# A mixture-of-experts stage: twelve of its 32 token tiles sent through DRAM to their two experts

## The reference, cut to what matters

```python
h = _layernorm(x) * (1 + ca) + sa                 # second layer
z = softmax(einsum('bse,he->bsh', h, W_A) * SCALING, axis=1)
out = causal_convolution(z, h @ W_V.T)            # per head, over all positions
x = x + ga * (out @ W_O.T + b_O)
h = _layernorm(x) * (1 + cb) + sb
weights = softmax(h @ gate_w.T)                   # 16 experts
top2_w, top2_idx = top_k(weights, 2)
y = relu(einsum('nh,edh->ned', h, expert_w) + expert_b)     # all 16 experts
x = x + gb * sum(take(y, top2_idx) * top2_w)                # two of them count
```

## Time and profile before

| | us |
|---|---|
| median of 3 runs | 1114.5 (1114.38 to 1114.91) |
| the profiled execution | 1114.68 |
| its span, first to last instruction | 1112.9 |
| mean granted clock of PE | 0.990 |

### The profile page before, as it was taken

The page is one execution under the profiler, slowest core; times in us unless marked ns, Lnnn a source line. Parts: engine busy times, 40 slices in busy tenths (PEclk is TensorE's granted clock), DMA queues, the critical chain, the costliest instruction groups (busy, mean ns, idle before and its releaser), DMA issues. The chain is left out here.

```text
span 1112.9 us, 34196 instructions
## 1 busy us (share of the span) xinstructions
PE 1034.9 (93%) x11851; PEld 716.1 (64%) x11851; DVE 870.4 (78%) x2888; ACT 840.4 (76%) x2673; POOL 735.5 (66%) x1184
## 2 busy tenths in 40 slices
PE   6889998799999999898899999998998999999995
PEld 3667764477777776565577777776565598854442
DVE  4999997588888888564788888887685653379998
ACT  5789984699999998433799999997355855478986
POOL 4999995699898897201888988987233220046775
PEclk9999999899999999999999999999999999899999
DMA  7000000112222221321112221221001444000000
GB/s 250 5 3 12 12 3 1 39 40 61 57 54 53 51 49 39 111 73 31 40 39 50 49 49 40 50 49 42 21 1 41 105 122 107 3 8 15 17 20 19
DMA packets 66509, 51.02 MB, mean 46 GB/s; under 512 B 42263, under 2 KB 53443, under 8 KB 66051
## 3 DMA queue, kind: packets, MB, share of 16 engines
q1 hardware_dynamic: 66339, 48.84, 17.3%
HBM read 21.41 MB, written 2.38 MB: 21 GB/s over the span
## 5 line engine op out<-in xcount | busy, mean ns | idle before, releaser
L1259 PE MATMUL psum<-wa_wqkv,wa_hT 128*128 128x512 f32 x384 | 189.0, 600 | 1.3 <-DVE wa_tmp L1124 1.3
L1216 ACT ACTIVATE wa_p<-psum,wa_nb 128x128 f32<-128x128 f32 x512 | 184.7, 403 | 0.0
L1105 POOL TENSOR_TENSOR wa_p<-wa_p,wa_rrs 128x512 f32<-128x512 f32 x128 | 133.4, 1042 | 10.1 <-DVE wa_rrs L1149 10.1
L1140 DVE CUSTOM_DVE_ANT_0 psum<-psum,wa_bias 128x128 f32<-128x128 f32 x512 | 132.5, 322 | 5.8 <-PE psum L1297 5.8
L1216 ACT ACTIVATION_READ_ACCUMULATOR wa_p<-psum,wa_nb 128x1 f32 x512 | 125.0, 244 | 0.0
L1997 ACT ACTIVATE cv_z_ex_yw<-psum,ex_w 128x128 f32<-128x128 f32 x384 | 106.9, 411 | 16.3 <-POOL ex_topf L1829 4.4
L2067 PE MATMUL psum<-ex_wc,ex_hT 128*128 128x512 f32 x256 | 115.8, 600 | 2.4 <-DVE cv_z_ex_yw L1932 1.4
L1081 POOL TENSOR_TENSOR wa_kr<-wa_kr,wa_tmp 128x512 f32<-128x512 f32 x64 | 81.7, 1276 | 41.6 <-DVE wa_tmp L1124 41.6
L1092 POOL TENSOR_TENSOR wa_qr<-wa_qr,wa_rn 128x512 f32<-128x512 f32 x64 | 66.8, 1044 | 56.3 <-ACT wa_rn L1198 56.3
L1226 ACT ACTIVATE wa_pT<-psum 128x512 f32<-128x512 f32 x128 | 78.3, 612 | 31.8 <-PE psum L1273 31.7
L1124 DVE TENSOR_TENSOR wa_tmp<-psum,wa_tabs 128x512 f32<-128x512 f32 x128 | 87.2, 681 | 0.0
(11 more groups left out here) (265 smaller groups left out, 3031.0 us busy)
## 6 DMA issues: line engine op xcount, KB each, us to landing
wa_vm<-wa_v SPq DMA_DIRECT2D x127, 128.0 KB, 2.4
cv_toep<-cv_zpad SPq DMA_DIRECT2D x32, 136.0 KB, 2.9
cv_toep<-cv_zpad SPq DMA_DIRECT2D x16, 264.0 KB, 4.4
wa_tabs<-in_rotations_dram SPq DMA_DIRECT2D x2, 2048.0 KB, 7.9
wa_rows<-y_rows SPq DMA_DIRECT2D x31, 128.0 KB
wa_rows<-y_rows SPq DMA_DIRECT2D x31, 127.0 KB
x_rows<-in_L_attn_x_dram SPq DMA_DIRECT2D x4, 512.0 KB, 5.6
out_dram<-x_rows SPq DMA_DIRECT2D x32, 64.0 KB, 1.5
```

The costliest lines, as they stand in the source:

```text
L1105: nc.gpsimd.tensor_tensor(p, p, cols_bc(rrs[:, t % 2, r, :], P), ALU.mult)\
L1140: m = nc.vector.tensor_tensor_reduce(out=s, in0=s, in1=edges, scale=-1.0, scalar=MAX_FLOAT, op0=ALU.add, op1=ALU.min, accum_out=nb[:, t % ...
L1216: e = nc.scalar.activation(pr[:, t % 2, r, h, :], sim_bank[r][:, P * h:P * h + P], ACT.Exp, bias=nb[:, t % 2, r, h:h + 1], scale=-1.0, acc ...
L1259: nc.tensor.matmul(bank, hT[:, t % 3, :], wqkv[:, INNER * k:INNER * k + INNER], start=True, stop=True).then_inc(done.sem, 1)
```

## The change

Tiles 0 to 11 (`SPARSE = 12`) no longer pass through all 16 experts. Each token is copied to two rows of a table in DRAM, one per chosen expert, the table is multiplied block by block with the expert that owns the block, and each token reads its two result rows back.

- POOL clears 35 semaphores at the start of the block (`ro.all`), makes constants (`fixed`), and normalises the twelve tiles in row form (`routed_rows`).
- PE turns those rows in convolution step 7 (`routed_turn`, 12 transposes) and multiplies them with the gate (`routed_gate`, 12 matmuls of 16 columns) into bank 7. To have them ready, `o_project` and `turn_o` of batch 0 are moved into steps 5 and 6, two groups each, all through bank 6.
- DVE takes top values and indices of the twelve tiles (`choose`, before it takes away the last convolution step) and marks them (`mark`). PE counts each token's rank in its expert (`ranks`, 13 matmuls), DVE turns it into a row number (`place`, 8 operations), into the expert of each block (`columns_of_weights`) and makes the two weights (`two_weights`).
- SP writes zeros over the table, 2.6 MB (`zero`). POOL sends the rows out in 24 indirect transfers (`scatter`, from step 9 of its phase). The table has 40 blocks of 128 rows, taken four at a time: 10 quads. SP fetches for each quad the rows in one transfer and the four expert matrices in four, each with a column number that it loads from SBUF into a register (`routed`), into three slots. PE transposes a quad, ACT copies it, PE multiplies it (four matmuls of 128x128), DVE takes relu times gb, SP stores the result. Two quads pass in each of the steps 17 to 21, between the dense `up` matmuls.
- POOL reads the results back in 24 indirect transfers (`gather`, from step 22, behind the store of all quads), DVE adds them with their weights (`sums`, steps 24 to 29).
- The dense experts have 20 tiles (12 to 31) instead of 32; `EARLY` is 2 instead of 6. The five choice stages of the dense tiles run on DVE, and the eight compares of a group are one.

The core of the diff:

```diff
+SPARSE = 12
+SCATTER_FROM, SCATTERS_PER = 9, 5
+QUADS_FROM, QUADS_PER = 17, 2
+GATHER_FROM, GATHERS_PER, SUM_LAG = 22, 2, 2
+        def routed(sp):
+            weights_ready(sp, 0)
+            sp.wait_ge(ro.v_meta, META_DONE)
+            sp.wait_ge(ro.scattered, 16 * 2 * SPARSE)
...
+            for q in range(NQ):
+                slot = q % ro.SLOTS
+                if q >= ro.SLOTS:
+                    sp.wait_ge(ro.p_up, q - ro.SLOTS + 1)
+                sp.dma_start(ro.rows_in[slot], rows[q]).then_inc(ro.fetched[slot], 16)
+                for i in range(4):
+                    at = sp.value_load(ro.column[0:1, 4 * q + i:4 * q + i + 1], min_val=0, max_val=(NE - 1) * E)
+                    sp.dma_start(ro.weights_in[slot][:, i, :], wc[:, 0, bass.ds(at, E)])\
+                      .then_inc(ro.fetched[slot], 16)
+                if q >= ro.SLOTS:
+                    result(q - ro.SLOTS)
...
+            def scatter(s):
+                for j, k in scatter_at.get(s, []):
...
+                    nc.gpsimd.indirect_dma_start(
+                        out=ro.hs, out_offset=bass.IndirectOffsetOnAxis(ap=ro.pos[:, j, k:k + 1], axis=0),
+                        in_=ro.y[:, j, :], in_offset=None).then_inc(ro.scattered, 16)
+            def gather(s):
+                for j in gather_at.get(s, []):
+                    if j == 0:
+                        gp.wait_ge(ro.stored, 16 * NQ)
...
-            return Phase([of(floats, 5), of(numbers_equal, 5), of(either, 5), of(masked, 6), of(weights, 6),
-                          (residual, UP_LAG + 2)], 0, TILES)
+            return Phase([(residual, UP_LAG + 2), step_from(scatter, SCATTER_FROM),
+                          step_from(gather, UP_LAG + 2)], 0, DENSE)
...
+            def quad_turn(n):
+                def f(s):
+                    for q in quads_at.get(s, [])[n:n + 1]:
+                        turn_bank_left(pe, "quad", q)
+                        pe.wait_ge(ro.fetched[q % ro.SLOTS], 80 * (q // ro.SLOTS + 1))
+                        for i in range(4):
+                            m = nc.tensor.transpose(h_bank[:, P * i:P * i + P], ro.rows_in[q % ro.SLOTS][:, i, :],
+                                                    c.ident[:, :])
+                        m.then_inc(ro.p_quad, 1)
+            def quad_up(n):
...
+                        pe.wait_ge(ro.a_quad, q + 1)
...
+                        for i in range(4):
+                            m = nc.tensor.matmul(bank[:, P * i:P * i + P], ro.turned[q % 2][:, i, :],
+                                                 ro.weights_in[q % ro.SLOTS][:, i, :], start=True, stop=True)
...
+            return Phase([(by_group(gate), 4), (up(0), UP_LAG), step_from(quad_turn(0), UP_LAG), (up(1), UP_LAG),
+                          step_from(quad_up(0), UP_LAG), (by_group(turn), 2), (up(2), UP_LAG),
+                          step_from(quad_turn(1), UP_LAG), (up(3), UP_LAG), step_from(quad_up(1), UP_LAG)], 0, DENSE)
...
-    EARLY, EX_STEPS = 6, TILES + 12
+    EARLY, EX_STEPS = NT - SPARSE - 2, TILES - SPARSE + 12
...
 # ACT, per convolution step s
+                    if s == QUADS + 2:
+                        on_scalar.scale(act, 0)
+                        o_columns(2)
+                        o_columns(3)
                     if s + 1 < STEPS:
                         for r in range(len(PARTS)):
                             lower_rows(s + 1, r)
                         values_now(s + 1)
...
+                    if s == QUADS + 2:
+                        on_scalar.scale(act, 1)
```

534 lines of the change are left out of this document (436 added, 98 removed).

## The result

| | before | changed |
|---|---|---|
| median, us | 1114.44 (4 runs, 1113.75 to 1114.91) | 1159.12 (4 runs, 1158.09 to 1161.17) |
| ratio | 1 | 1.0404 (95% interval 1.0386 to 1.0422) |
| span of the profiled execution, us | 1112.9 | 1157.4 |
| mean granted clock | 0.990 | 0.966 |
| T, end of DVE's last addition of batch 1 | 979.0 | 998.8 |

The forecast was 1121.0 with a range up to 1143. The sign was right, the size was not: 44.7 us slower instead of 6.5. T came 19.8 us later, where I had 18.9. The error lies behind T: 158.6 us instead of 121.3. I go through the profile after in order of time.

A forecast was written before the change was run, and what follows sets the result against it. PE and DVE were taken to bound the dense experts together, within 0.1 us a tile. From 1114.7 us, 20.3 less behind the output stretch, 18.9 more ahead, 3.1 and 4.6 for transfers: 1121.0 us, range 1103 to 1143.

The forecast's parts named there:

- terms of step 6: Ahead of T, convolution step 6: PE waits 4.4 us before `o_project(3)` for DVE's addition, behind ACT's `scale(1)`.
- the stretch to T: The output stretch, up to DVE's last addition of batch 1: 20.3 us forecast, 18.4 before the change.
- The stand: PE's wait before `o_project(3)` in convolution step 6, put down to ACT's order of work: 4.4 us.
- the clock: Ahead of T: PE's wait in step 6 should let its clock fall from 2.4 to 1.2 GHz, costing 4 us (0 to 5).
- the part "Transfers": Behind T: POOL late by 3.1 us with its gathers, and PE waiting 4.6 us for quads that SP fetches.
- my own sign: PE's waits on transfers summing to over 15 us would show the prediction wrong in its mechanism.
- SP's quad, 4.6 us: SP spends 4.6 us issuing each quad's transfers and register loads, where PE wants one every 3.75 us.
- The third rival: SP starves the quads: at 0.9 us a load a quad costs 6.6 us, the last 24.5 us late, 1141; chance 0.17.
- Scatter and gather at 1.1 us each: POOL's time per indirect transfer; 15 scatters go by T + 10, the other nine by T + 27, landed T + 29.5.
- The first relu at T + 8.3: Behind T: about 35 small operations and two of 640 elements stand before the first dense tile's relu, 8.3 us.
- Gathers, 3.1 us: A step's four gathers (4.4) and residual (1.0) on POOL against DVE's 4.8; POOL 3.1 us late by the sixth step.
- The fourth rival: DVE's halvings slow POOL's transfers: a gather costs 1.9 us, the sixth step is 22 us late, 1140; chance 0.10.

The follow-up runs named there:

- free_transfers: The changed kernel with the scatters, the register loads (fixed columns instead) and the gathers left out, all waits kept: 1118.1 us, 1.0068 to the kernel before.

## Why the prediction was wrong

**What held, and how far.** Ahead of T: 18.9 us forecast, 19.8 measured, with the terms of step 6 (4.86 for 4.4), gate (2.85 for 2.9), `place` (2.96 for 2.6) and the stretch to T (20.8 for 20.3). These are right one by one; the agreement of the sums is in part luck. T itself varies by more than 10 us between profiles. The terms listed add up to 14.3 and not 13.4 (ACT's copy, 0.85, is not in the sum). The stand had a second cause of the same size. And the clock did not cost 4 us: PE worked at 0.50 from 959.0 to about 963.6, by my estimate 2.3 us, and in the stretch behind it stood better than before. For the clears, the block's memset on POOL, of the kernel before and of the changed one:

```profile
851.12 0.20 POOL L2179 MEMSET cv_zeros<- 32x128 f32 x1 [8.97 <-POOLq L1686]
```

```profile
852.33 0.19 POOL L2568 MEMSET cv_zeros<- 32x128 f32 x1 [11.76 <-issue]
```

POOL's idle time ahead of it is 2.8 us longer, where I took 1.5, but the memset starts only 1.2 us later; how much of that reaches PE is not shown. Behind T, without transfers: 113.6 us forecast, 115.5 in free_transfers; a step with two quads took 6.8 to 7.9 us (7.5), a step with sums 4.77 (4.7). (PE's pace of 3.8 us a tile does not follow from the earlier trace rows, where 9.09 us for 20 records are 3.6 for eight; it agrees with the last of the earlier trace rows, 121.16 us over 32 tiles.) That the saving of twelve dense tiles, 46.7 us, is nearly all paid back by the quads, the late start, the sums and what lies ahead of T was the sound part: free transfers give 1118.1, and the prediction without its transfers was 1113.3.

**What failed is the part "Transfers".** I gave it 3.1 + 4.6 = 7.7 us; it measures 158.6 - 115.5 = 43.1. By my own sign, PE's waits on transfers over 15 us (19.7), that is a wrong mechanism and not only a size. By its steps:

- *SP's quad, 4.6 us.* It is 6.24. The load was taken as 0.4 + 0.1 and is 0.62; the weight transfer was taken as 0.33, from SP's store of a tile, and is 0.63. The row beside it in the same group, `wa_rows<-y_rows` at 0.645, was the nearer one, for it copies from SBUF to SBUF, as the weight transfer does. The third rival had the right mechanism, and I gave it 0.17. Its 6.6 us a quad came near by two errors against each other: its load was too dear (0.9), its weight transfer too cheap. Its 24.5 us were PE's waits, which measure 19.7; that leaving the loads out gives 24.3 back, the clock with it, is a coincidence.
- *Scatter and gather at 1.1 us each.* 0.96 + 0.30 = 1.26 for a scatter. Fifteen before the residual as forecast, but "the other nine go by T + 27" took the residuals as ready; they wait for the first tile, and that was late by the stand. First quad fetched at T + 39.8 instead of T + 30.
- *The first relu at T + 8.3.* The chain was sized right (8.5 undisturbed) and delayed by 7.5 us by the unbroken row of scatters (8.5 without them and with pauses between them). No rival had this: all of them asked what the transfers cost the engines that issue them, none what they cost the others.
- *Gathers, 3.1 us.* 8.8 us. A step of POOL is 6.2 to 7.5 us instead of 5.4.

Singly left out, the scatters give 21.0 us (158.6 - 137.6), the loads 24.3 and the gathers 8.4, together 53.7. They give 43.1 together, so 10.6 us are counted twice: quads that are fetched earlier and quads that are fetched faster save the same waits of PE.

The Trainium skill ("SBUF — State Buffer", section "SBUF: two separate sides") says that GpSimd cannot write the descriptors of its transfers while DVE runs an operation in its two-port mode. Whether the halvings are such operations no run here shows. The fourth rival asked for that effect. The scatters beside DVE's halvings (1023 to 1030 us) took 0.95 to 1.61 us, the median of all 24 being 0.96, and the gathers 0.94 to 1.96 with a median of 0.99: a delay now and then, not a tripling. The dearer effect went the other way, from POOL's transfers to the signals of DVE.

**Chances.** Slower had 0.60, and the range ended at 1143, just above the single prices of the third and fourth rival, 1141 and 1140. Bad ends of several unknown costs can come true together: with SP at 6.6 and the gathers at 1.9 us the sum of the forecast's own terms would have been 1121 + 19.9 + 18.9 = 1160. That it meets the measured 1159 is chance, since the gathers cost 8.8 and the stand is not in it. Costs that no row shows, in four places one behind another, should have had a range that adds the ends.

## What to carry to other kernels

Work that is cut from two engines in balance is only won if what replaces it has an issuer with time to spare: here 46.7 us of dense tiles were bought with 24 + 24 indirect transfers on POOL and 40 loads with transfers on SP, each around 1.25 us, one behind another. Count issues times period for each queue first, and compare with the pace at which the consumer wants them. Where a price is in no row, take it from the row that has the same direction and pattern, not the cheapest one, and let the upper ends add in the range. Then ask what a burst of transfers does to engines that never wait for it, and what bulk writes share the way with a prefetch.
